# Output stage: third and fourth k tiles in buffers of their own, banks copied out one by one, tile work split 5, 7, 4

## The reference, cut to what matters

```python
xn = _layernorm(x, axis=-1)
s = _L0_attn_ref(xn, ...)      # ends with: out = einsum('bli,di->bld', yn, out_proj_w)
...
H_res = sinkhorn_log(H_res_logits)            # 4x4 per token, 50 rounds
H_res = (1.0 - g) * I + g * H_res
x_mixed = jnp.einsum('btij,btjc->btic', H_res, x_streams)
y_distributed = jnp.einsum('btc,btn->btnc', y, H_post)
g = _silu(x_mixed + y_distributed)
x = x + s * g
```

## Time and profile before

| | before |
|---|---|
| median of 3 runs | 3055.89 us |
| profiled execution, its own time | 3054.47 us |
| its span, first to last instruction | 3053.0 us |
| output stage (from 2345 us to the end) | 708 us |
| PE busy, whole span | 3000.2 us (98%) |
| DVE busy, whole span | 2128.1 us (70%) |
| ACT busy, whole span | 1763.6 us (58%) |
| POOL busy, whole span | 687.7 us (23%) |
| memory traffic | 444.90 MB, mean 146 GB/s |

### The profile page before, as it was taken

How to read it: one execution, slowest core, us unless ns; L and a number is a source line. 1 busy time by engine, 2 the same in 40 slices (tenths; PEclk the granted TensorE clock), 3 DMA queues, 4 the chain that set the end, 5 groups by cost and what they waited for, 6 DMA issues and landing times.

```text
span 3053.0 us, 45217 instructions
## 1 busy us (share of the span) xinstructions
PE 3000.2 (98%) x14352; PEld 2341.8 (77%) x14352; DVE 2128.1 (70%) x2648; ACT 1763.6 (58%) x3728; POOL 687.7 (23%) x575
## 2 busy tenths in 40 slices
PE   8999999999999998999999999999999999999998
PEld 7777777777777777777777777777777788887787
DVE  7667667576666685767666666766667878677877
ACT  5667575757666575576665757575665332234443
POOL 4222213121222134413222231212124000001112
PEclk9999999999999999999999999999999999999999
DMA  3534343443434353435243433434254444456665
GB/s 138 169 126 158 108 159 107 141 138 110 155 110 155 114 197 98 157 121 172 95 168 104 157 123 135 139 109 160 90 171 153 148 138 150 146 196 211 209 212 182
DMA packets 125532, 444.90 MB, mean 146 GB/s; under 512 B 17488, under 2 KB 21712, under 8 KB 109008
## 3 DMA queue, kind: packets, MB, share of 16 engines
q1 hardware_dynamic: 117552, 423.14, 41.1%
q0 software_dynamic: 4096, 14.68, 1.2%
q10 hardware_dynamic: 3744, 5.51, 0.6%
HBM read 397.86 MB, written 45.42 MB: 145 GB/s over the span
## 4 chain that ended last, share of the span: by engine, by line
PE 82%; issue 5%; DVE 4%; POOL 2%; ACT 2%; DMA 2%; DVEq 0%; SPq 0%; ACTq 0%; POOLq 0%
PE bank L1101 18%; PE bank L1103 17%; PE bank L1102 17%; PE bank L1139 9%; PE bank L1361 5%; PE bank L1362 5%; PE bank L1363 5%; PE bank L1113 2%; PE bank L1125 2%; DMA acc<-in_w_out 1%; PE bank L1149 1%; POOL gate L467 1%; DVE acc L839 1%; DVE x_lo L1356 1%; DVE x_lo L1355 1%
## 5 line engine op out<-in xcount | busy, mean ns | idle before, releaser
L1101 PE MATMUL bank<-x_hi,w_hi 128*128 128x512 f32 x2576 | 1024.6, 398 | 2.4 <-DVE acc L839 2.4
L1103 PE MATMUL bank<-x_hi,w_lo 128*128 128x512 f32 x2576 | 1003.0, 389 | 0.0
L1102 PE MATMUL bank<-x_lo,w_hi 128*128 128x512 f32 x2576 | 1000.9, 389 | 0.0
L839 DVE SCALAR_TENSOR_TENSOR acc<-bank,conv_w,acc 128x511 f32<-128x511 f32 (+2 forms) x576 | 430.8, 748 | 270.5 <-ACT acc L616 241.9
L1101 PEld LDWEIGHTS bank<-x_hi,w_hi 128*128 128x128 f32 x2576 | 484.1, 188 | 114.7 <-issue 22.2
L1103 PEld LDWEIGHTS bank<-x_hi,w_lo 128*128 128x128 f32 x2576 | 484.0, 188 | 102.6
L1102 PEld LDWEIGHTS bank<-x_lo,w_hi 128*128 128x128 f32 x2576 | 484.9, 188 | 93.6
L616 ACT ACTIVATE acc<-bank,tap_par 128x512 f32<-128x512 f32 x192 | 149.5, 779 | 517.0 <-PE bank L1103 486.0
L1361 PE MATMUL bank<-x_hi 128*128 128x512 f32 x1008 | 394.7, 392 | 8.9 <-DVE x_lo L1356 5.3
L1362 PE MATMUL bank<-x_lo,x_hi 128*128 128x512 f32 x1008 | 393.1, 390 | 0.0
L1363 PE MATMUL bank<-x_hi,x_lo 128*128 128x512 f32 x1008 | 392.9, 390 | 0.0
(11 more groups left out here) (165 smaller groups left out, 3408.0 us busy)
## 6 DMA issues: line engine op xcount, KB each, us to landing
units<-cum_scratch SPq DMA_DIRECT2D x128, 1280.0 KB, 6.7
w_raw<-in_w_in SPq DMA_DIRECT2D x160, 512.0 KB, 3.7
w_raw<-y_scratch SPq DMA_DIRECT2D x128, 512.0 KB, 3.6
y_scratch<-gate SPq DMA_DIRECT2D x32, 1024.0 KB, 6.5
acc<-in_w_out SPq DMA_DIRECT2D x128, 256.0 KB, 3.8
xbc<-in_x SPq DMA_DIRECT2D x16, 512.0 KB, 5.6
units<-in_x SPq DMA_DIRECT2D x16, 512.0 KB, 3.7
rstd_b<-rc_scratch SPq DMA_DIRECT2D x32, 256.0 KB, 4.3
```

The source lines that it names most:

```text
L839: dve.scalar_tensor_tensor(acc[:, s % 2, back:], bank_proj[s % 2][:, 0:SEQ - back], mix.conv_w[:, at, m, 3 - back:4 - back], acc[:, s % 2, ...
L1101: pe.matmul(out, w_hi[m % 2][:, k, :], hi, start=(k == 0), stop=False)
L1102: pe.matmul(out, w_hi[m % 2][:, k, :], lo, start=False, stop=False)
L1103: mm = pe.matmul(out, w_lo[m % 2][:, k, :], hi, start=False, stop=(k == KT - 1))
```

## The change

The change does four things.
- K tiles 2 and 3 (i = 1 of pass 0) are loaded into spare parts of the `units` buffers 2 and 0, with semaphores `ahead_loaded`. Their loads wait for `multiplied`, which frees those buffers. Raw buffers 0 and 1 then hold only k tiles 0 and 1 before k tiles 4 and 5, whose loads need `k_split` of 1 and 2 (before: 3 and 4).
- SP issues the loads of k tiles 4 and 5 ahead of the whole drain, where before they stood between the drain's last steps. K tile 6 still follows the drain.
- PE signals each of the first seven banks of a pass's last k tile (`each=bank_done`). ACT copies banks 0 to 3 and DVE banks 4 to 7, each as soon as it has ended; in pass 2 bank t also waits for product t with `s_sb`.
- `F_PARTS` becomes 5, 7, 4, 0.

```diff
         for j in range(2):
+            sp.wait_ge(multiplied, UNITS * HALVES * GROUPS - 2 + j)
             output.load(sp, 0, 1, j)
-        drain(piece, HALVES - 1, SLOTS, min(LAST.store))
         for j in range(2):
             output.load(sp, 0, 2, j)
-            drain(piece, HALVES - 1, min(LAST.store) + j, min(LAST.store) + j + 1)
+        drain(piece, HALVES - 1)
...
+        spare = [mix.units[:, 2 * SPAN * b:2 * SPAN * b + DM + 512] for b in (2, 0)]
+        self.y_ahead, self.w_ahead = [b[:, 0:DM] for b in spare], [b[:, DM:] for b in spare]
         self.k_loaded = [sem("k_loaded0"), sem("k_loaded1")]
+        self.ahead_loaded = [sem("ahead_loaded0"), sem("ahead_loaded1")]
...
+    def ahead(self, p, i):
+        return p == 0 and isinstance(i, int) and i == 1
+
+    def raw(self, p, i, j):
+        return (self.y_ahead[j], self.w_ahead[j]) if self.ahead(p, i) else (self.y_raw[:, j, :], self.w_raw[:, j, :])
+
     def load(self, sp, p, i, j):
-        need(sp, self.k_split, OT * p + 2 * i + j - 1)
-        sp.dma_start(self.y_raw[:, j, :], self.d["y"][p // 2, 2 * i + j]).then_inc(self.k_loaded[j], 16)
-        sp.dma_start(self.w_raw[:, j, :], self.d["w_out"][p % 2, 2 * i + j]).then_inc(self.k_loaded[j], 16)
+        loaded = self.ahead_loaded[j] if self.ahead(p, i) else self.k_loaded[j]
+        if p == 0 and isinstance(i, int) and i == 2:
+            sp.wait_ge(self.k_split, j + 1)
+        elif not (p == 0 and isinstance(i, int) and i < 2):
+            sp.wait_ge(self.k_split, OT * p + 2 * i + j - 1)
+        y, w = self.raw(p, i, j)
+        sp.dma_start(y, self.d["y"][p // 2, 2 * i + j]).then_inc(loaded, 16)
+        sp.dma_start(w, self.d["w_out"][p % 2, 2 * i + j]).then_inc(loaded, 16)
...
-    def products(self, pe, p, i, j, tiles=range(NT), first=False, last=False, done=True):
+    def products(self, pe, p, i, j, tiles=range(NT), first=False, last=False, done=True, each=None):
         pe.wait_ge(self.k_split, OT * p + 2 * i + j + 1)
         for t in tiles:
             if first and p:
-                pe.wait_ge(self.evacuated[t % 2], NT // 2 * (p - 1) + t // 2 + 1)
+                by, place = divmod(t, NT // 2)
+                pe.wait_ge(self.evacuated[by], NT // 2 * (p - 1) + place + 1)
             mm = self.product(pe, p, i, j, t, first, last)
+            if each is not None and t < NT - 1:
+                mm.then_inc(each, 1)
...
-    F_PARTS = ((0, 6), (6, 14), (14, NS * NS), (0, 0))
+    F_PARTS = ((0, 5), (5, 12), (12, NS * NS), (0, 0))
+
+    def bank_ended(eng, p, t):
+        if t < ENDED:
+            eng.wait_ge(bank_done, ENDED * p + t + 1)
+        else:
+            eng.wait_ge(k_done, OT * (p + 1))
+        if p == 2:
+            eng.wait_ge(s_mul, t + 1)
...
         def evacuate(p):
-            act.wait_ge(k_done, OT * (p + 1))
             if p == 0:
                 all_stored(act)
-            if p == 2:
-                act.wait_ge(s_mul, NT)
-            for t in range(0, NT, 2):
+            for t in range(NT // 2):
+                bank_ended(act, p, t)
                 act.activation(s_sb[:, t, (p % 2) * 512:(p % 2 + 1) * 512], bank[t][:, :],
                                ACT.Copy).then_inc(evacuated[0], 1)
...
         def evacuate(p):
-            dve.wait_ge(k_done, OT * (p + 1))
             if p == 0:
                 all_stored(dve)
-            if p == 2:
-                dve.wait_ge(s_mul, NT)
-            for t in range(1, NT, 2):
+            for t in range(NT // 2, NT):
+                bank_ended(dve, p, t)
                 dve.tensor_copy(s_sb[:, t, (p % 2) * 512:(p % 2 + 1) * 512], bank[t][:, :]).then_inc(evacuated[1], 1)
```

More of the change, by code:

```diff
@@ L1323, in __init__ @@
         self.w_lo = [[mix.x_lo[:, i, 512 * n:512 * (n + 1)] for i in range(2)] for n in range(2)]
+        spare = [mix.units[:, 2 * SPAN * b:2 * SPAN * b + DM + 512] for b in (2, 0)]
+        self.y_ahead, self.w_ahead = [b[:, 0:DM] for b in spare], [b[:, DM:] for b in spare]
         self.k_loaded = [sem("k_loaded0"), sem("k_loaded1")]
+        self.ahead_loaded = [sem("ahead_loaded0"), sem("ahead_loaded1")]
         self.k_hi, self.k_split, self.k_done = sem("k_hi"), sem("k_split"), sem("k_done")
-        self.evacuated = [sem("evacuated_even"), sem("evacuated_odd")]
+        self.evacuated = [sem("evacuated_low"), sem("evacuated_high")]
     def pair(self, p, i):
@@ L1332, in reused @@
         return not (p == 0 and isinstance(i, int) and i < 2)
+    def ahead(self, p, i):
+        return p == 0 and isinstance(i, int) and i == 1
+    def raw(self, p, i, j):
+        return (self.y_ahead[j], self.w_ahead[j]) if self.ahead(p, i) else (self.y_raw[:, j, :], self.w_raw[:, j, :])
     def load(self, sp, p, i, j):
-        need(sp, self.k_split, OT * p + 2 * i + j - 1)
-        sp.dma_start(self.y_raw[:, j, :], self.d["y"][p // 2, 2 * i + j]).then_inc(self.k_loaded[j], 16)
-        sp.dma_start(self.w_raw[:, j, :], self.d["w_out"][p % 2, 2 * i + j]).then_inc(self.k_loaded[j], 16)
+        loaded = self.ahead_loaded[j] if self.ahead(p, i) else self.k_loaded[j]
[6 more added lines that the diff above has]
+        sp.dma_start(w, self.d["w_out"][p % 2, 2 * i + j]).then_inc(loaded, 16)
     def split_hi(self, act, p, i, j):
         kk = OT * p + 2 * i + j
-        act.wait_ge(self.k_loaded[j], 32 * ((OT // 2) * p + i + 1))
+        if self.ahead(p, i):
+            act.wait_ge(self.ahead_loaded[j], 32)
+        elif p == 0 and isinstance(i, int) and i == 0:
+            act.wait_ge(self.k_loaded[j], 32)
+        else:
+            act.wait_ge(self.k_loaded[j], 32 * ((OT // 2) * p + i))
         if self.reused(p, i):
@@ L1345, in split_hi @@
         n = self.pair(p, i)
-        act.activation(self.y_hi[n][j], self.y_raw[:, j, :], ACT.Copy)
-        act.activation(self.w_hi[n][j], self.w_raw[:, j, :], ACT.Copy).then_inc(self.k_hi, 1)
+        y, w = self.raw(p, i, j)
+        act.activation(self.y_hi[n][j], y, ACT.Copy)
+        act.activation(self.w_hi[n][j], w, ACT.Copy).then_inc(self.k_hi, 1)
     def split_lo(self, dve, p, i, j):
@@ L1354, in split_lo @@
         n = self.pair(p, i)
-        dve.tensor_tensor(self.y_lo[n][j], self.y_raw[:, j, :], self.y_hi[n][j].bitcast(F32), ALU.subtract)
-        dve.tensor_tensor(self.w_lo[n][j], self.w_raw[:, j, :], self.w_hi[n][j].bitcast(F32), ALU.subtract).then_inc(self.k_split, 1)
+        y, w = self.raw(p, i, j)
+        dve.tensor_tensor(self.y_lo[n][j], y, self.y_hi[n][j].bitcast(F32), ALU.subtract)
+        dve.tensor_tensor(self.w_lo[n][j], w, self.w_hi[n][j].bitcast(F32), ALU.subtract).then_inc(self.k_split, 1)
     def product(self, pe, p, i, j, t, first=False, last=False):
@@ L1420, in output_programs @@
     LAG = 5
+    ENDED = NT - 1
     TURNS = OT // 2 - 3
@@ L1702, in run_vector @@
         for t in range(NT):
-            dve.wait_ge(bank_done, t + 1)
+            dve.wait_ge(bank_done, ENDED * (PASSES - 1) + t + 1)
             dve.tensor_tensor(f_keep[:, t, :], f_keep[:, t, :], bank[t][:, :], ALU.mult).then_inc(last_mul, 1)
@@ L1719, in run_tensor @@
                 products(pe, p, OT // 2 - 1, 0)
-                products(pe, p, OT // 2 - 1, 1, last=True)
+                products(pe, p, OT // 2 - 1, 1, last=True, each=bank_done)
         pe.wait_ge(output.k_split, OT * PASSES - 1)
```

## The result

The changed kernel takes 3067.15 us (median of 6 runs, 3065.84 to 3071.35), the kernel before on the same chip 3055.97 us (6 runs). The ratio is 1.0036, 95% interval 1.0026 to 1.0046: 11.2 us slower, which is more than the 0.2% that can be told from no change. The forecast was 3062.6, the range 3052 to 3068. The profiled execution took 3066.48 us with a span of 3065.0, 12.0 more than before in both.

A forecast was written before the change was run, and what follows sets the result against it. PE, busy 98% of the span, was taken as the bound, so only its idle time could be won. Terms 0 + 1.0 - 1.9 + 4.4 - 0.5 + 2.9 + 0.8 = +6.7 gave 3062.6 us, range 3052 to 3068.

The forecast's parts named there:

- The turns of pass 2: Six turns between k tiles 5 and 29: two added steps ahead of the tanh lengthen them, 5 by 0.81 and 0.3, +4.4.
- Turns neutral: Rival, 0.15: DVE's eight steps, not the landing, start the split of 4i+3; 0.8 saved, 0.8 added; 3054.5.
- Landing moves: Rival, 0.16: contention sets k tile 6's landing, before 2361.6; stalls go, 4i+3 lands 0.8 sooner; 3050.2.
- Landing later: Rival, 0.14: load of 4i+4, issued 0.4 us sooner, makes 4i+3 land 0.4 later; 13 turns give +5.2, 3067.8.
- Ends of passes: Ends of passes 0 and 1: PE's gaps for ACT's copy close, 2 by -0.94, -1.9.
- the end of pass 2: ACT waits only for `f_silu`, but two more steps stand ahead; of the 1.88 gap 0.5 is taken back.
- K tile 6 and the clock: Output stage's start: k tile 6 still lands at 2365.5, gain 0; half clock after a 3.5 us stall, +1.0.
- My own upper bound: Start of the stage, +1: k tile 7's load, issued some 1.5 us sooner, takes bandwidth from k tile 6.
- the full price: Clock drop behind k tile 6's stall: nine matmuls by 0.2, 1.9 us, of which the forecast took 1.0.
- Pass 3: Seven turns: 7 by 0.8, 5.6 added, less 1.7 of lead and about 1.0 in the last three; +2.9.

## Why the prediction was right, and where not

**The turns of pass 2: right, in size and mechanism.** +4.6 for +4.4. From the rounding of 4i+3 to the end of the turn, five turns grew by 0.77 to 0.81 us, and the one in which the load had landed early by 0.37, where the step had 0.81 and 0.3; the landings add another 0.3 over the six. DVE's idle time ahead of the split of 4i+3, the two steps behind it and the queue order of ACT stand in the timelines as the step put them, and the moved tanh shows that the order is the cause. At the ends of five of the six PE idles 0.92 to 0.95 us for DVE's split, at the sixth 0.35.

**"Turns neutral" and "Landing moves": fell.** Turns are 23.2 us long on average, not 22.4, and k tile 6 was rounded at 2367.10.

**"Landing later" names 3067.8, close to what was measured, and is still not what happened.** In pass 2 the rounding of 4i+3 starts on average 6.86 us into a turn before and 6.90 after (each tanh's start, less 4.35 or 5.15). The rival wanted 0.4 more in every turn.

**Ends of passes: right.** -0.94 each, to the hundredth. At the end of pass 2 I took -0.5 and it was -1.1; the copies alone made it -1.3 (2.11 to 0.77), so the two steps seem to cost 0.2 to 0.3 there and not most of what the copies give. Even that isn't clear: with the new copies and the old shares the wait was 0.78 from start to start in one kernel (the changed one with 6, 8, 2) and 1.08 in another (k tile 6 between the stores), and the changed kernel's is 1.02. With the old copies PE's idle time there was between 1.35 and 2.74 us in four kernels, so this term is known to about a microsecond only.

**K tile 6 and the clock: the step that was mis-sized.** I took 0 for the start and 1.0 for the clock; it was +0.8 and +2.3. The place in SP's queue was read rightly: 29.5 us lie between the restart of the earlier trace rows and k tile 6 in five kernels with the new loads (29.51 to 29.98), 28.7 to 28.9 in four without. K tile 6 was issued 17.5 us behind the restart both times (2358.65 less 2341.16, before 2357.90 less 2340.39), but it was rounded 8.45 us behind its issue in place of 7.61. My own upper bound gave a reason, k tile 7's load 1.84 us behind that of k tile 6 where it was 3.09. In the five kernels the rounding comes 8.45 to 8.47 us behind the issue and k tile 7's load 1.84 or 1.85 behind it, in the four it is 7.60 to 7.99 with 3.08 to 3.38. No run changed that distance alone, so the cause is argued only. For the clock I had halved nine matmuls' worth, as one row spoke for a drop and one against; a stall of 4.15 us is far beyond both, and eleven matmuls ran slow. The Trainium skill (TensorE: Matmul & The Clock Gate, What's actually happening) has the clock set by how busy the engine has lately been, which spoke for the full price, and the trace agrees so far that a drop followed the stall, at 2.3 us.

The step also said that a stall of 3.5 us is longer than any here. That holds for the output stage only. In the mixer of the kernel before, PE idles 5.11 us ahead of 1166.73 and 2.63 us ahead of 1183.24, and the windows behind both read half clock:

```profile
1166.73 1.09 PE L1171 MATMUL bank<-ident,xbc 128*128 128x128 f32 x4 [5.11 <-DVE x_lo L923]
...
1183.24 0.85 PE L1171 MATMUL bank<-ident,xbc 128*128 128x128 f32 x4 [2.63 <-DVE x_lo L923]
```

```profile
1167.00:1169.00 2.00, 2.00 (x8) 0.95 (x8) 0.18 (x1) 1.09 (x2) 1.67 (x5) 0.50 0.27 31
1184.00:1186.00 2.00, 2.00 (x11) 2.00 (x10) 1.97 (x5) 1.42 (x3) 1.52 (x3) 0.50 0.04 1
```

With these rows beside the earlier trace rows the full price was the better estimate for 3.5 us of idle.

**Pass 3: the step that failed.** +5.9 for +2.9. I had put 5.6 into the chain, and taken off 1.7 for its lead over PE and 1.0 for three turns in which PE held the chain. The lead was eaten as said (1.7 before, 0.2 now, 3037.03 to 3037.20). But the seven turns grew from 152.3 to 159.4, by 7.1. From the rounding of 4i+3 to the end of a turn they grew by 5.9, as the steps want it, so the 1.0 that I took off was not to be had: once the chain is behind, PE no longer holds it. Another 0.4 comes ahead of the first of these turns, which starts 5.09 us behind PE's first matmul of the pass in place of 4.73. The last 1.2 is late landings, two above all, where the roundings come 8.86 and 8.38 us into turns of 23.96 and 23.47. Two others are at 6.20 and 6.36. In pass 3 these scatter by 2.7 us, and that was in none of my terms.

**The mixer's 0.8** stands in no term, and no part of the change explains it. The restart of the earlier trace rows lies between 2340.21 and 2340.94 in the four kernels without the new loads and between 2340.43 and 2342.32 in the nine with them. The two ranges overlap, each is from single executions, and whether the loads cost something in the drain stays open.

In sum, the direction and the main mechanism held; 4.5 of the 5.3 us that were missing come from the clock, the late k tile and pass 3, less the 0.6 won at the end of pass 2, and the last 0.8 are the mixer's. The time lies outside the 3058 to 3066 over which I spread the forecast and 0.85 us inside the end of the range, which had been drawn for the rival of later landings; that it holds the time is in part luck. A slowdown that can be told from no change had 0.45, no more than no change itself (0.46).

## What to carry to other kernels

Before work is spread more evenly over an engine, look for who waits for the last piece, and what unrelated work is queued behind that waiter: here two steps of 0.41 us on DVE cost 11 us in 14 turns, because ACT's tanh stood ahead of a rounding that PE needed. Moving the waiter behind that rounding was worth more than any share of the steps. And when a load is moved ahead to close a stall, move the first load that is then late: two that were not the last to be late went ahead, the stalls merged into one, and the clock fell behind it.

## What the runs showed of the hardware

PE's stalls in the output stage were followed by a half-clock stretch after 2.91, 2.74, 4.15, 4.98 and 5.27 us of idle, for seven to fourteen matmuls, and after 2.19 us at the end of pass 2 with the shares alone, but not after 2.49, 2.45 and 2.25 us ahead of k tile 6 (the kernel before, the shares alone, and before with the tanh moved). So the length of the last stall alone does not say whether the clock falls. The restart of the earlier trace rows shows it best: in thirteen profiled executions PE idles 1.16 to 1.22 us there behind the same one-column matmuls, and in seven of them seven to nine matmuls at half clock follow, 1.4 to 1.7 us dearer, in six none. In the same seven the clock had fallen near 1185 us in the mixer, in the six near 1176. What decides it was not isolated.

The landing of one and the same pair of loads varied by 2.7 us from turn to turn while two pieces of x and POOL's transfer ran beside it. With the x pieces queued behind the pair, the rounding came within 0.05 us of the same place in each of the six turns of pass 2.

DVE's split of the y half took 1.21 to 1.23 us wherever POOL computed nothing beside it. The last one of a turn, k tile 4i+5, took 2.80 to 2.81 in all six turns of pass 2, in the kernel before and in the changed one, and each began while POOL added x to a tile. In the turn of the changed kernel shown above:

```profile
2735.82 2.40 POOL L1541 TENSOR_TENSOR th<-bc,th 128x1024 f32<-128x1024 f32 x1 [16.37 <-DVE bc L1698]
```

```profile
2736.50 2.81 DVE L1377 TENSOR_TENSOR x_lo<-w_raw,x_hi 128x1024 fp32r<-128x1024 f32 x1 [0.76 <-ACT x_hi L1368]
```

These 1.6 us stand in the chain of each turn, twice as much as the two steps. No run moved POOL's addition, so that it is the cause is not shown.
